# Attention 1 of a two-layer transformer: projections as three fp32r products of split operands, and sums of squares by ScalarE's accumulator

## The reference, cut to what matters

```python
def _L1_attn_ref(x, w_qkv, w_o, qn_g, qn_b, kn_g, kn_b):   # H, HKV, D = 16, 4, 128; S = 256
    qkv = jnp.einsum('bsh,oh->bso', x, w_qkv)
    q, k, v = jnp.split(qkv, [H * D, (H + HKV) * D], axis=-1)
    ...
    q = _layernorm(q, qn_g, qn_b)      # over each head's 128 features
    k = _layernorm(k, kn_g, kn_b)
    q = q * cos + _rotate_half(q) * sin
    k = k * cos + _rotate_half(k) * sin
    ...
    scores = jnp.einsum('bhqd,bhkd->bhqk', q, k) / jnp.sqrt(jnp.float32(D))
    scores = jnp.where(causal, -jnp.inf, scores)
    weights = jax.nn.softmax(scores, axis=-1)
    attn = jnp.einsum('bhqk,bhkd->bhqd', weights, v)
    return jnp.einsum('bsd,od->bso', attn, w_o)
```

## Time and profile before

| | us |
|---|---|
| median of 3 runs (911.09 to 912.24) | 911.41 |
| the profiled execution, whole | 909.07 |
| its span | 907.3 |

### The profile page before, as it was taken

One profiled execution on the slowest core, in us unless ns is written; L12 is line 12 of the kernel. 1 busy time (PEld: TensorE's weight loads), 2 busy tenths in 40 slices (PEclk: granted clock), 3 DMA queues, 4 the chain that ended last, 5 costly groups with the idle time before them and its releaser, 6 DMA issues.

```text
span 907.3 us, 12347 instructions
## 1 busy us (share of the span) xinstructions
PE 764.7 (84%) x3984; PEld 557.9 (61%) x3984; DVE 692.2 (76%) x1162; ACT 462.6 (51%) x992; POOL 338.1 (37%) x242
## 2 busy tenths in 40 slices
PE   6770569867898987799999999999955799999997
PEld 2240446544533653566767676677743689999996
DVE  4897689889748976999999899999877554444443
ACT  1743558630337312667667666756732354444442
POOL 1001356532330522134323333332443286666663
PEclk9685669998899998999999999999987899999999
DMA  5340133335030212011111111201300243344331
GB/s 172 125 162 30 70 115 118 117 117 220 1 98 0 94 33 84 24 36 59 36 47 36 59 36 36 68 27 42 112 0 1 97 141 139 139 140 140 141 134 46
DMA packets 28883, 74.63 MB, mean 82 GB/s; under 512 B 3632, under 2 KB 6336, under 8 KB 28448
## 3 DMA queue, kind: packets, MB, share of 16 engines
q1 hardware_dynamic: 28384, 71.51, 22.8%
q10 hardware_dynamic: 448, 2.49, 0.8%
HBM read 72.55 MB, written 1.44 MB: 82 GB/s over the span
## 4 chain that ended last, share of the span: by engine, by line
PE 59%; DVE 15%; ACT 11%; issue 10%; POOL 3%; DMA 1%; POOLq 0%; DVEq 0%; ACTq 0%; SPq 0%
PE ps L1678 8%; PE ps L1794 6%; PE ps L1795 6%; PE ps L1796 6%; PE ps L1759 4%; PE ps L1638 4%; PE ps L1747 3%; PE ps L1442 3%; DVE hS L981 3%; PE ps L1658 3%; PE ps L1728 2%; PE ps L1415 2%; ACT dA L605 2%; DVE ps L973 2%; PE ps L1423 1%
## 5 line engine op out<-in xcount | busy, mean ns | idle before, releaser
L403 POOL TENSOR_TENSOR hS<-hS,BCb 128x512 f32<-128x512 f32 x64 | 81.6, 1278 | 131.4 <-issue 67.3
L1394 DVE SCALAR_TENSOR_TENSOR arena<-ps,arena 128x1024 f32<-128x1024 f32 x32 | 39.2, 1225 | 102.1 <-ACT arena L847 93.1
L426 POOL TENSOR_TENSOR hS<-hS,BCb 128x1024 f32<-128x1024 f32 x23 | 56.1, 2441 | 107.5 <-DVE ps L973 93.4
L1678 PE MATMUL ps<-WB,hT 128*128 128x512 f32 x192 | 88.0, 603 | 3.1 <-DVE arena L1267 2.1
L476 POOL TENSOR_TENSOR MHl<-arena,MHh 128x1024 fp32r<-128x1024 f32 x34 | 81.8, 2405 | 17.0 <-ACT MHh L850 17.0
L1423 PE MATMUL ps<-ident,hS 128*128 128x128 f32 x256 | 39.9, 311 | 54.1 <-POOL hS L426 47.5
L1794 PE MATMUL ps<-Wh,MHh 128*128 128x256 f32 x272 | 77.8, 286 | 5.9 <-POOL MHl L476 5.9
L1011 DVE TENSOR_TENSOR_SCAN hS<-dA,ps 128x512 f32<-128x512 f32 x64 | 78.1, 1220 | 2.2
L1795 PE MATMUL ps<-Wl,MHh 128*128 128x256 f32 x272 | 77.6, 285 | 0.0
L1796 PE MATMUL ps<-Wh,MHl 128*128 128x256 f32 x272 | 77.6, 285 | 0.0
L1423 PEld LDWEIGHTS ps<-ident,hS 128*128 128x128 f32 x256 | 32.9, 160 | 64.6 <-POOL hS L426 53.7
(11 more groups left out here) (233 smaller groups left out, 1966.2 us busy)
## 6 DMA issues: line engine op xcount, KB each, us to landing
BCb<-bc_dram SPq DMA_DIRECT2D x32, 512.0 KB, 3.6
BCb<-bcq_dram SPq DMA_DIRECT2D x64, 256.0 KB, 3.2
arena<-gate_dram SPq DMA_DIRECT2D x32, 512.0 KB, 3.6
WB<-in_we SPq DMA_DIRECT2D x34, 256.0 KB, 2.7
WB<-in_wqkv SPq DMA_DIRECT2D x1, 3072.0 KB, 12.8
WA<-in_wo ACTq DMA_DIRECT2D x1, 2048.0 KB, 7.8
WA<-in_ffn SPq DMA_DIRECT2D x1, 1408.0 KB, 7.8
pkb<-in_pk SPq DMA_DIRECT2D x2, 698.0 KB, 4.7
```

Of the source, the lines that this page charges most:

```text
L403: gp.tensor_tensor(h, h, qbc(q)[:, 1:2, :].broadcast_to([P, DT, S]), ALU.mult).then_inc(s["c_ready"], 1)
L426: gp.tensor_tensor(h, h, BCb[g % SB_LOADS][:, 1:2, :].broadcast_to([P, DT, HALF]), ALU.mult).then_inc(s["c_ready"], 1)
L1678: last = mm(ps[:, bank + t, :], hT[:, c, P * (2 * b + t):P * (2 * b + t) + P], WB[:, c, c0:c0 + 512], start=(c == 0), stop=(c == HC - 1))
```

## The change

Products: the normalised hidden state and the six 512-column blocks of the QKV weights are each split in a high part rounded to fp32r and a low part (the rest, also fp32r). `project` makes each product as high x high + high x low + low x high, 12 fp32r products instead of 4 fp32 products. The parts are made by `w1_high` (ScalarE, 6 copies of 128x1024: after the feed-forward steps j = 2, 7, 10 and after the exponentials of SSM steps 6, 7, 8), `w1_low` (GpSimd, 6 subtractions of 128x1024, between its SSM products), `hidden_high` (ScalarE, in place of its copy to `hT`) and `hidden_parts` (VectorE: one copy, as before, and two new subtractions of 128x512 for each half).

Sums of squares: `job_sq` becomes two steps, `sq0` and `sq1`, each with four squares of 128x128, whose accumulator output is the sum of one head. `job_sum` is gone; GpSimd's 1/sqrt (plan entry `rstd`) waits for `job_sq` alone, and so do `rot` and `banks_free`, for both steps.

Order: the exponentials `da` move behind `ptc`; `sq0` stands where `sq` stood, ahead of `pt` and `ptc`, and `sq1` behind `ptc` and `da`. The planner loses the cost of `sum`, and a projection costs 2.6 in place of 3.4.

Room: the parts take memory of the SSM's rings. The ring of 8 quarters becomes 6 for `hS`, 4 for `dA` and 6 for the broadcasts, exponentials are issued two steps ahead in place of three, and `ln_apply(4)` waits for the last projection since the parts lie over `H` and `hT`.

```diff
-QRING = 8
+HRING, DRING, BRING = 6, 4, 6
@@ gpsimd
+            def w1_low(k):
+                n = W1_ORDER[k]
+                pool.wait_ge(s["w1_hi"], k + 1)
+                w = WB[:, :, 512 * n:512 * n + 512]
+                gp.tensor_tensor(W1l[:, :, 512 * n:512 * n + 512], w, W1h[n][:].bitcast(F32), ALU.subtract).then_inc(s["w1_lo"], 1)
+
             zero_cols(1, 0)
-            zero_cols(1, 1)
-            for q in range(8):
+            w1_low(0)
+            w1_low(1)
+            for q in range(2):
+                times_cq(q)
+            w1_low(2)
+            for q in range(2, 8):
                 times_cq(q)
             ln_rstd(3, (0,))
             for q in range(8, Q_IN_FFN):
                 times_cq(q)
+            w1_low(3)
+            w1_low(4)
             ln_rstd(3, (1,))
+            w1_low(5)
             def job(j):
-                pool.wait_ge(s["job_sum"], j + 1)
+                pool.wait_ge(s["job_sq"], 2 * j + 2)
+                if j >= 2:
+                    pool.wait_ge(s["job_rope"], 8 * (j - 1))
@@ scalar
+            def hidden_high(hf):
+                act.wait_ge(s["ln_tr_mm"], 8 + 2 * hf + 2)
+                sc.copy(H1h[hf][:, 0, :], ps[:, TR_BANK[2][hf], :]).then_inc(s["ln_tr_act"], 1)
+
+            def w1_high(k):
+                n = W1_ORDER[k]
+                if n == W1_V:
+                    act.wait_ge(ld["wqkv1"], 16)
+                else:
+                    act.wait_ge(s["w1_centered"], HC)
+                if k >= 2:
+                    act.wait_ge(s["delta_ready"], 4)
+                sc.copy(W1h[n][:], WB[:, :, 512 * n:512 * n + 512]).then_inc(s["w1_hi"], 1)
...
-            def job_sq(j):
+            def job_sq(j, t):
                 act.wait_ge(s["job_mm"], j + 1)
                 if j:
-                    act.wait_ge(s["job_sum"], j)
-                k = job_bank(j)
-                sc.activation(job_s(j), ps[:, k:k + 2, :], ACT.Square).then_inc(s["job_sq"], 1)
+                    act.wait_ge(s["job_sq"], 2 * j + t - 1)
+                if j >= 2:
+                    act.wait_ge(s["job_rstd"], j - 1)
+                for h in range(REP1):
+                    c = slice(D1 * h, D1 * h + D1)
+                    last = sc.activation(SQ[:, t, c], ps[:, job_bank(j) + t, c], ACT.Square, accum_out=jst[:, j % 2, 0, REP1 * t + h:REP1 * t + h + 1])
+                last.then_inc(s["job_sq"], 1)
@@ vector
+            def hidden_parts(hf):
+                dve.wait_ge(s["ln_tr_mm"], 8 + 2 * hf + 2)
+                k, z = TR_BANK[2][hf], slice(512 * hf, 512 * hf + 512)
+                ch.step(v.tensor_copy(H1h[hf][:, 1, :], ps[:, k + 1, :]))
+                dve.wait_ge(s["ln_tr_act"], 4 + hf + 1)
+                v.tensor_tensor(H1l[:, 0, z], ps[:, k, :], H1h[hf][:, 0, :].bitcast(F32), ALU.subtract)
+                ch.wait()
+                v.tensor_tensor(H1l[:, 1, z], ps[:, k + 1, :], H1h[hf][:, 1, :].bitcast(F32),
+                                ALU.subtract).then_inc(s["ln_tr_dve"], 1)
@@ vector, job and job_sum
-                dve.wait_ge(s["job_sq"], j + 1)
+                dve.wait_ge(s["job_sq"], 2 * j + 2)
...
-                v.tensor_reduce(jst[:, j % 2, 0, :], job_s(j).rearrange("p t (h d) -> p (t h) d", d=D1), AX.X, ALU.add).then_inc(s["job_sum"], 1)
@@ tensor, project
+                pe.wait_ge(s["w1_lo"], W1_ORDER.index(n) + 1)
                 for t in range(2):
                     for c in range(HC):
-                        last = mm(ps[:, bank + t, :], hT[:, c, P * (2 * b + t):P * (2 * b + t) + P], WB[:, c, c0:c0 + 512],
-                                  start=(c == 0), stop=(c == HC - 1))
+                        a = P * (2 * b + t)
+                        high, low = H1h[b // 2][:, c, a % HALF:a % HALF + P], H1l[:, c, a:a + P]
+                        o, wh, wl = ps[:, bank + t, :], W1h[n][:, c, :], W1l[:, c, 512 * n:512 * n + 512]
+                        mm(o, high, wh, start=(c == 0), stop=False)
+                        mm(o, high, wl, start=False, stop=False)
+                        last = mm(o, low, wh, start=False, stop=(c == HC - 1))
@@ att1_plan
-    cost = {"rot": 2.6, "sum": 1.2, "rope": 3.2, "step": 2.0}
+    cost = {"rot": 2.6, "rope": 3.2, "step": 2.0}
-        if m + 3 < QSTEPS:
+        if m + 2 < QSTEPS:
-    pe = {"proj": 3.4, "v": 3.4, "tr": 0.45}
+    pe = {"proj": 2.6, "v": 2.6, "tr": 0.45}
-        plan += [p for p in now if p[0] == "da"] + pick("vc", "sq")
+        plan += pick("vc", "sq0")
         if ok(u - 1):
             plan += [("pt", u - 1), ("ptc", u - 1)]
-        plan += pick("wo1", "rope", "rot", "sum")
+        plan += [p for p in now if p[0] == "da"]
+        plan += pick("sq1", "wo1", "rope", "rot", "rstd")
```

More of the change, by code:

```diff
@@ L100, in build @@
         X = sb("X", [P, NT, HID])
+        hidden_base = nc.sbuf_base
         H = sb("H", [P, NT, HID])
         hT = sb("hT", [P, HC, T])
+        ctx_base = -(-nc.sbuf_base // 32) * 32
         ctxp = sb("ctxp", [P, B, S + DC - 1])
+        pk_base = -(-nc.sbuf_base // 32) * 32
         pkb = sb("pkb", [P, PK_N])
@@ L129, in qbc @@
         def qbc(q):
-            k = q % QRING
+            k = q % BRING
             flat = BCb[k // 2][:].rearrange("p r t -> p (r t)")
@@ L140, in split, with part @@
             return nc.alloc_sbuf_tensor_at(name, shape, F32R, offset=scan_base + place * DT * T * 4)
+        def part(name, shape, offset):
+            return nc.alloc_sbuf_tensor_at(name, shape, F32R, offset=offset)
+        w1_homes = [pk_base, scan_base + 4 * DT * T * 6 + 4096, scan_base + 4 * DT * T * 4,
+                    scan_base + 4 * DT * T * 4 + 4096, scan_base + 4 * DT * T * 7 + 4096 * 3, ctx_base]
+        W1h = [part(f"W1h{n}", [P, HC, 512], w1_homes[n]) for n in range(6)]
+        H1h = [part(f"H1h{hf}", [P, HC, HALF], hidden_base + 4096 * hf) for hf in range(2)]
+        H1l = part("H1l", [P, HC, T], hidden_base + 4 * NT * HID)
         hTh, hTl = split("hTh", 0, [P, HC, T]), split("hTl", 1, [P, HC, T])
@@ L162, in build @@
         dsc = sb("dsc", [P, HID])
+        wb_base = nc.sbuf_base
         WB = sb("WB", [P, HC, NQ1 + 2 * NK1])
@@ L265, in build @@
         ld_bc = [sem(f"ld_bc{s}") for s in range(SB_LOADS)]
-        ld_bq = ld_bc + [sem(f"ld_bq{s}") for s in range(SB_LOADS, QRING)]
-        bq_base = [16 * LAYER_STEPS // SB_LOADS] * SB_LOADS + [0] * (QRING - SB_LOADS)
-        bq_count = lambda q: bq_base[q % QRING] + 16 * (q // QRING + 1)
+        ld_bq = ld_bc + [sem(f"ld_bq{s}") for s in range(SB_LOADS, BRING)]
+        bq_base = [16 * LAYER_STEPS // SB_LOADS] * SB_LOADS + [0] * (BRING - SB_LOADS)
+        bq_count = lambda q: bq_base[q % BRING] + 16 * (q // BRING + 1)
         ld_we = [sem(f"ld_we{s}") for s in range(WRING)]
@@ L373, in _ @@
             sp.wait_ge(s["out_done"], 32)
+        W1_V, W1_K = 5, 4
+        W1_ORDER = [W1_V, W1_K, 0, 1, 2, 3]
         @block.gpsimd
@@ L462, in _ @@
             for kind, a in ATT1_PLAN:
-                if kind == "sum":
+                if kind == "rstd":
                     job(JOB[a])
@@ L742, in _ @@
                     d_u(3)
+                if j in W1_AT:
+                    w1_high(W1_AT.index(j))
                 if j in FFN_SSM_AT:
@@ L810, in _ @@
                     act.dma_start(WO1, io["wo1"]).then_inc(ld["wo1"], 16)
-                elif kind == "sq":
-                    job_sq(JOB[a])
+                elif kind in ("sq0", "sq1"):
+                    job_sq(JOB[a], int(kind == "sq1"))
                 elif kind == "trc":
@@ L1248, in _ @@
             ln_stats(3, 1)
-            ln_tr_copy(2, 0)
+            hidden_parts(0)
             ln_apply(3, 1)
@@ L1309, in _ @@
                 elif kind == "ln1":
-                    ln_tr_copy(2, 1)
-                elif kind == "sum":
-                    job_sum(*a)
+                    hidden_parts(1)
                 elif kind == "rope":
@@ L1328, in _ @@
                 ln_stats(4, hf)
+            dve.wait_ge(s["job_mm"], len(JOB))
+            dve.wait_ge(s["v_mm"], B)
             for hf in both:
@@ L1872 @@
 FFN_SSM_AT = [9, 11]
+W1_AT = [2, 7, 10]
+W1_AFTER = [6, 7, 8]
 PREP_XDBL, PREP_DT = 1, 3
@@ L1890, in rope_job @@
         at(slot, "proj", (b, i))
-        at(slot, "sq", (b, i))
+        for t in range(2):
+            at(slot, f"sq{t}", (b, i))
         at(slot + 1, "rot", (b, i))
-        at(slot + 1, "sum", (b, i))
+        at(slot + 1, "rstd", (b, i))
         at(slot + rope, "rope", (b, i))
@@ L1916, in att1_plan @@
             v_job(u + 12, b + 1)
-    cost = {"rot": 2.6, "sum": 1.2, "rope": 3.2, "step": 2.0}
-    ssm = [("da", (m, d)) for m in range(Q_IN_FFN, Q_IN_FFN + 3) for d in range(DT)]
+    cost = {"rot": 2.6, "rope": 3.2, "step": 2.0}
+    ssm = [("da", (m, d)) for m in range(Q_IN_FFN, Q_IN_FFN + 2) for d in range(DT)]
     for m in range(Q_IN_FFN, QSTEPS):
-        if m + 3 < QSTEPS:
-            ssm += [("da", (m + 3, d)) for d in range(DT)]
+        if m + 2 < QSTEPS:
```

(3 more changed lines are left out.)

42 lines of the change are left out of this document (19 added, 23 removed).

## The result

| | before | after |
|---|---|---|
| median of 5 runs, us | 911.41 (909.56 to 912.24) | 916.31 (915.18 to 916.58) |
| the profiled execution, whole | 909.07 | 916.57 |
| its span | 907.3 | 914.8 |
| mean granted clock | 0.923 | 0.917 |

The ratio is 1.0062, with a 95% interval of 1.005 to 1.0074: slower by 0.6%, little but clear of the noise, where -14.2 us had been forecast.

A forecast was written before the change was run, and what follows sets the result against it. TensorE and VectorE were taken as both nearly full, with ScalarE in the loop. Terms -7.6 - 1.0 - 1.9 - 1.5 - 2.2 = -14.2 us took 911.4 to 897.2 us; range 889 to 914.

The forecast's parts named there:

- the start: Stretch up to the fifth unit of attention 1: forecast 2.2 us shorter through missing sums and shorter projections.
- the steady part: Attention 1 from unit 5 to unit 63, 273.4 us before: forecast 12.0 us shorter.
- weight splits: ScalarE casts and GpSimd subtractions in idle time: forecast to cost nothing; without that cover, 6 x 1.05 us of ScalarE at most.
- Projections: 24 projections on TensorE: 12 fp32r products in 2.75 us instead of 3.43, saving 0.68 each, 16.4 us in all.
- P: Slot of attention 1's three-slot loop that holds the projection: 6.89 us before, forecast 5.81.
- The rival of closer products: TensorE products closer than 0.229 us, so VectorE sets the period: at most 11 us less, 886; chance 0.02.
- The two rivals built on a slower one (912 and 926): ScalarE squares at 0.35 us, 912 in all, chance 0.12; at 0.45 ScalarE becomes the loop, 926, chance 0.14.
- R: First slot of attention 1's three-slot loop: 3.27 us before, forecast the same, about 4.1 with two `da`.
- `rot` can start at 7.6 in place of 7.4: Rotary products on VectorE in a plain period: start 0.2 us later but end before VectorE is wanted.
- T: Slot after R in attention 1's three-slot loop: 4.00 us before, forecast to stay 4.00.
- `da` behind `ptc`: ScalarE order: frees 0.4 us at the head of P; five periods with two `da` gain about 0.2 each, 1.0 in all.
- The clock rival: Idle stretch of 4.70 us before transposes grows about 1.5; TensorE's lower clock costs 2 to 5 us, 901; no separate chance.

The follow-up runs named there:

- e4: Changed kernel with fp32 projections and no splits of weights or hidden state; accumulator squares, order and smaller rings stay; 919.66 us.
- e2: Changed kernel with a job's three rotary multiplications split by PSUM bank into six, the first three waiting for the first half's squares only; 909.59 us.
- e11: Changed kernel with fp32 projections, no splits, whole-bank squares and sums back on VectorE, leaving only its order and smaller rings; 910.34 us.
- e10: Changed kernel with only `da` put ahead of the squares again in slots with a rotary projection; 907.07 us.
- e3: Changed kernel with five of GpSimd's six weight subtractions at later times and the third ScalarE cast two places later; 907.15 us.
- e8: Changed kernel with the moves of e3 and e2, squares cut three and five, and `da` ahead of squares in rotary-projection slots; 892.66 us.
- e9: Changed kernel with only the last three weight subtractions moved, until VectorE has finished the last layer norm before attention 1; 912.72 us.

## Why the prediction was wrong, point by point

Two sums fell short: the start by 11.5 us (+9.3 for -2.2), the steady part by 8.0 (-4.0 for -12.0). Three steps failed: the weight splits that "cost nothing", the order of `da`, and the end of `rot` that nobody was said to want.

**Projections: right.** 12 products at 0.23 us, P 5.82 where 5.81 was forecast; worth 11.5 us in the steady part (e4 to after). The rival of closer products falls, and with it, for this stream of fp32r products, the Trainium skill's 131 ns (TensorE: Matmul & The Clock Gate, section Back-to-back issue gap): the trace shows 230.

**Squares: right in size,** 0.25 to 0.26 us each. The two rivals built on a slower one (912 and 926) had the wrong reason; the time that came has another cause.

**When they start: off by 0.2.** I let ScalarE begin when TensorE's next work began. The squares begin 5.28 us after P and not 5.08: the last product starts at 469.46, the next work at 469.69, ScalarE at 469.89. It was so in before. The prediction put TensorE's next work at 444.89, which is the end of the last product; it starts at

```profile
444.73 0.60 PE L1442 MATMUL ps<-ident,hS 128*128 128x128 f32 x4
```

and ScalarE 0.20 us later, at 444.93. The projection's 3.43 us are right all the same, since both their ends were read 0.16 late, but the tail between TensorE and ScalarE got lost. By the rows it makes most of R's 0.24 us; no run tests it apart.

**"`rot` can start at 7.6 in place of 7.4, but ends before VectorE is wanted": the step that failed in T.** I asked when VectorE was wanted and not who waits for `rot`. The transposes of the job before write the same two banks. 0.35 us in 13 slots, 4.9 us with what hangs on it (e2).

**`da` behind `ptc`: right at P, the wrong sign where `da` meets squares.** The 0.4 us at the head of P were saved (P 6.48 in e4 and e11, 6.89 in before). But I priced a slot with two `da` at R 4.1 and -0.2 a period; it measured R 4.30 and T 4.35, +0.3 a period, in four periods. Above all the comparison was incomplete: ahead of `sq0` they would have lain in the 2.1 us for which ScalarE waits for the projection. 6.4 us (e10).

**Weight splits, "cost nothing": the largest miss.** The cover that I named (idle GpSimd) was there, and the price "if it is gone" was ScalarE's casts. The work was hidden on its own engine and charged to another. Some 10 us with the slow clock that followed (e3), against -2.2 for the start.

**The clock rival came true in part.** The idle stretch that it named, ahead of the first transposes, grew from 4.70 to 6.55 us, as it said. Two more came that it hadn't named: 5.74 us ahead of the first projection (0.95 in the earlier trace rows, 2.14 in e3), for the most part by the subtractions, and 3.22 in the second slot (2.13 in before). By an estimate from the rows (products and transposes at twice their spacing) the lower clock cost 6.1 us there against 2.7 in before, 3.4 more; the rival had 2 to 5. It was a share of the loss and not its source.

**Hidden state's splits, smaller rings: right,** as far as e11 and e3 show: with fp32 projections rings and order cost nothing, and with the subtractions moved the start is 1.4 us shorter than before. The wait ahead of the first projection is 1.2 us longer there (2.14 and 0.95), where +1.3 was forecast for the hidden state's splits.

**VectorE** lost 11 us of busy time, not 22: of 24.2 for the sums, 2.7 came back as splits, and about 8.5 as instructions that stood still under GpSimd's and count as busy. That leaves 13.0, which is what the durations fell by; the busy time, which counts overlapping records once, fell by 11.3.

Of the signs I named, one came in full (`pv` waits for `ptc`) and two in part: R over 4 us, but in the periods with `da` and not in plain ones, and a scan that waits for exponentials, once, 2.03 us. The granted clock in the middle stayed at 1.00. The steady part of 261.4 us that was forecast is passed, but only with two repairs that the forecast didn't know it needed: 258.0 in e8.

What stays open: R at 3.51. A rotary product that doesn't wait for the squares at all wasn't tried, since both engines would read one bank. Open too is why the lower clock lasted for none, six or 12 products after the same wait.

## What to carry to other kernels

Work put in the idle time of GpSimd isn't free while VectorE runs instructions with all inputs in SBUF: look at what VectorE does in just those microseconds, and put the work where it reads PSUM or waits. When an instruction is made longer, list every semaphore and every bank that hangs on its end, not only the next instruction of its queue. And before moving work behind a critical step, look whether its old place lay in a wait that is there anyway.

## What the runs showed of the hardware

- GpSimd's subtractions and products and many VectorE instructions with all inputs in SBUF exclude each other: L1009 went from 1.23 us to 3.25, L1055, which writes PSUM, from 0.70 to 1.26, four L1091 from 1.38 to 6.37, and a subtraction of 128x16 on GpSimd took 0.97 in place of 0.22. Instructions with an input in PSUM kept their times inside such a stretch (L1286 0.68, the scan L1064 1.22).
- It is no rule for all that lies in SBUF: eight MAX8 of VectorE (715.58, 0.84 us together) ran inside a subtraction of the experts (715.43, 2.38 us), and four L1091 took 1.35 us beside GpSimd's L410 of 128x4, but 3.01 a moment later (240.83) beside its products of 128x256.
- A held instruction counts as busy in the profile. A group whose mean rises with no change to it is the sign: L1091 took 1.38 us for its four alone and 3.22 with a subtraction beside.
- A square of 128x128 with accumulator costs ScalarE 0.25 us from start to start, also with its accumulator read (0.19 to 0.27) in the rows: the read overlaps the next square.
- TensorE's fp32r products of 512 columns start 0.43 us apart at the lower clock (granted 0.50) and 0.23 at the upper (1.00); in the change the former held for 14 products after 5.74 us of idle time. After 3.22 us of idle time it held for six there, for 12 in e9 and for none in e3.
- ScalarE starts on a PSUM bank 0.20 us after TensorE's next work starts, and 0.43 after the last product into the bank, at the upper clock (469.46, 469.69, 469.89).
